# Attention core: one software pipeline per head pair in place of one per block of 256 queries

## The chip, the cores and the metric

The kernel runs as one program on all 8 cores of one Trainium2 chip. Each core works alone on two of the 16 sequences. The metric is the device time of the slowest core in microseconds, the median over several executions.

## What is computed

Three layers act on x, 16 sequences of 2048 x 1024, float32: `x + 0.5*ffn(layernorm(x))`, then `x + attn(layernorm(x))`, then `x + 0.5*ffn(layernorm(x))` with the same ffn weights. The ffn is itself an attention without a mask over 4 of 16 heads that a router picks. The change is in `attn`, differential attention with a causal mask:

```
q = rotary(rmsnorm(x @ Wq.T)); k = rotary(rmsnorm(x @ Wk.T))   # 16 heads of 64
v = x @ Wv.T                                                    # 8 heads of 128
attn = softmax(causal(q @ k.T / 8))                             # 2048 x 2048 for each of 16 heads
attn = attn[head 2h] - lam * attn[head 2h+1]                    # 8 pairs
out  = layernorm(attn @ v) * (1 - LAMBDA_INIT)
return out @ Wproj.T
```

## The kernel before

Five queues of instructions are written out in Python, one for each engine: `pe` (TensorE, the matmuls), `act` (ScalarE, the exponentials), `dve` (VectorE), `gps` (GpSimd) and `sp` (SyncE, which issues DMAs here). Each engine works through its own queue in order. What ties them together are counting semaphores: `P.wait("pe", self.ACT, n)` puts into TensorE's queue a wait until ScalarE has finished its n-th instruction, and everything behind that wait in TensorE's queue waits too.

For each of the two sequences a core runs the stages: load and layernorm, ffn, q/k/v projection, `emit_attn_core`, the output projection with the next layernorm, ffn again. `emit_attn_core` is the stage that the change touches.

It loops over the NH = 8 pairs p of heads. For each pair:

- SyncE loads the transposed q and k of the pair and its v strip, one pair ahead, into one of two halves (`issue_pair_loads`).
- The 2048 queries are cut into 8 blocks of 256, `qh` = 0 to 7. Because of the causal mask, block qh needs the keys of 2qh+2 tiles of 128, taken two tiles at a time: it has qh+1 groups g. So a pair has 1+2+...+8 = 36 groups, and the stage has 2 x 8 x 36 = 576 in all.
- One group is three steps. `emit_scores(g)`: TensorE writes the scores of 2 heads x 2 key tiles x 256 queries into one of two PSUM tiles, `pbig[g % 2]` (4 matmuls, and 4 short ones more that add the mask in the last, diagonal, group of a block). `emit_exp(g)`: one ACTIVATE on ScalarE turns these 1024 columns into probabilities in slot g % 4 of `big_b`. `emit_av(g)`: TensorE multiplies them with v (8 matmuls of 129 columns, 6 in the diagonal group) and accumulates in the banks `obs`, of which there are two sets that take turns from block to block.
- The order within a block is a pipeline two groups deep: scores 0, scores 1, exp 0, and then for each g: exp g+1, av g, scores g+2. Scores g+2 waits for exp g, which frees the PSUM tile. At the end of a block the pipeline runs empty: the next block's scores 0 stand in TensorE's queue behind av of the last group, and that waits for the last exp.
- After the block's last av, VectorE does the fixup (lines 1022 to 1038: two reciprocals, a scaling, and for each of two query tiles the difference of the two heads and its statistics). The av of the block after next waits for it (`fixup_ms`), since it writes the same banks. In every pair but the first, the first fixup also waits until the pair before has been stored (`store_ms`), since both use `zstrip`.
- At the end of a pair ScalarE computes 1/sqrt(var) (L1043, L1045), VectorE normalises 16 tiles (L1050), and SyncE stores them to `zhat_d`. ScalarE's first exp of the next pair stands behind L1045 in its queue.

In the profile's lines L954 is the score matmul, L963 the mask matmul, L974 the exp, L995 the av matmul.

Of the kernel before, what the change touches and what calls it, by code (L numbers as in the profile page):

```python
# [76 lines left out]
class MK:  # L77
# [823 lines left out]
    def emit_attn_core(self, b):  # L901
        P = self
# [15 lines left out]
        store_ms = None  # L918
        for p in range(NH):
# [9 lines left out]
            first_fix_of_pair = True  # L929
            for qh in range(8):  # L930
                o = qh % 2
                obs = (self.pb[2 * o], self.pb[2 * o + 1])
                oput = [0, 0]
                nkt = 2 * qh + 2
                ngroups = nkt // 2
                n_out = [0, 0]
                for kt in range(nkt):
                    for qi in range(2):
                        if 2 * qh + qi >= kt:
                            n_out[0] += 1  # L940
                            n_out[1] += 1

                def emit_scores(g):
                    kts = (2 * g, 2 * g + 1)
                    pw = self.pbig[g % 2]
                    P.wait("pe", self.ACT, exp_ms[g % 2])
                    diag = [(ki, qi) for ki, kt in enumerate(kts)
                            for qi in range(2) if 2 * qh + qi == kt]
                    for hi in range(2):
                        last_of_all = (hi == 1)  # L950
                        for ki, kt in enumerate(kts):
                            is_last = (not diag) and (ki == 1)
                            P.pe(lambda e, kt=kt, ki=ki, hi=hi, pw=pw, qh=qh,
                                 qT=qT, kT=kT, is_last=is_last: e.matmul(  # L954
                                pw[:, hi * 512 + ki * 256:hi * 512 + (ki + 1) * 256],
                                kT[hi * 64:(hi + 1) * 64, kt * 128:(kt + 1) * 128],
                                qT[hi * 64:(hi + 1) * 64, qh * 256:(qh + 1) * 256],
                                start=(ki == 0), stop=is_last,
                                tile_position=(hi * 64, 0)),
                                inc=(is_last and last_of_all))  # L960
                        for di, (ki, qi) in enumerate(diag):
                            is_last = (di == len(diag) - 1)
                            P.pe(lambda e, pw=pw, hi=hi, ki=ki, qi=qi, is_last=is_last: e.matmul(  # L963
                                pw[:, hi * 512 + ki * 256 + qi * 128:hi * 512 + ki * 256 + (qi + 1) * 128],
                                self.ident_bf, self.diag_bf,
                                start=False, stop=is_last),
                                inc=(is_last and last_of_all))
                    return self.PE.n

                def emit_exp(g, pe_ms):  # L970
                    pw = self.pbig[g % 2]
                    P.wait("act", self.PE, pe_ms)
                    P.wait("act", self.PE, av_ms.get(("pt", g % 4), 0))
                    P.act(lambda e, pw=pw, g=g: e.activation(  # L974
                        out=self.big_b[:, (g % 4) * 1024:(g % 4) * 1024 + 1024],
                        in_=pw[:, 0:1024], func=AF.Exp, scale=0.125, bias=self.neg8_col))
                    exp_ms[g % 2] = self.ACT.n
                    return self.ACT.n

                def emit_av(g, act_ms):  # L980
                    kts = (2 * g, 2 * g + 1)
                    P.wait("pe", self.ACT, act_ms)
                    if oput[0] == 0:
                        P.wait("pe", self.DVE, fixup_ms[o])
# [265 lines left out]
```

How the kernel before makes its waits and increments, by code:

```python
    def wait(self, eng, sem, val):  # L173
        if val > 0:
            self.q[eng].append(lambda e, s=sem, v=val: e.wait_ge(s.h, v))
# [15 lines left out]
    def dma(self, queue, out, in_, **kw):  # L191
        ch = self._chan(queue)
        v0 = ch.n
        self.on(queue, lambda e, o=out, i=in_, s=ch, w=v0, kw=kw: (
            e.wait_ge(s.h, w), e.dma_start(out=o, in_=i, **kw).then_inc(s.h, 16)))
        return ch, ch.inc(16)
# [1 line left out]
    def dmat(self, queue, out, in_):  # L198
        ch = self._chan(queue)
        v0 = ch.n
        self.on(queue, lambda e, o=out, i=in_, s=ch, w=v0: (
            e.wait_ge(s.h, w), e.dma_start_transpose(o, i).then_inc(s.h, 16)))
        return ch, ch.inc(16)
# [8 lines left out]
        def step(e, f=fn, s=sem, w=w):  # L212
            e.wait_ge(s.h, w)
            f(e).then_inc(s.h, 1)
# [12 lines left out]
    def pe(self, fn, inc=True):  # L227
        if inc:
            self.on("pe", lambda e, f=fn, s=self.PE: f(e).then_inc(s.h, 1))
            return self.PE.inc(1)
        self.on("pe", fn)
        return self.PE.n
```

## Time and profile before

| | |
|---|---|
| median of 3 runs | 4290.23 us (4281.84 to 4294.78) |
| the profiled execution | 4281.57 us |
| span of its slowest core, core 1 | 4280.0 us; all cores 4251.3 to 4280.0 us |
| busy on core 1: TensorE, ScalarE, VectorE | 2549.3 us (60%), 1468.1 us (34%), 1446.2 us (34%) |
| mean granted TensorE clock, core 1 | 0.684 of 2.4 GHz |
| attention core, first exp to end of last exp, core 1 | 967.8 to 1569.3 us and 3100.5 to 3688.8 us |
| exps in it (L974) | 576, 641.7 us busy, 673.6 us of idle time before them |

The profile is of the slowest core. A row of it gives an engine, a line, what the instruction writes and reads, how many there were, and the idle time of the engine just before them with what ended it. The granted clock is 1.00 or 0.50 (2.4 or 1.2 GHz) nearly everywhere; it is the share of TensorE's clock that the chip let through in that stretch.

### The profile page before, as it was taken

The page shows a single profiled execution, that of the slowest core. Times are in us where ns is not written, and L with a number is a line of the kernel's source. Part 1 is how long each engine was busy: PE and PEld are TensorE (multiplying, and loading weights), DVE is VectorE, ACT ScalarE, POOL GpSimd, SP SyncE. Part 2 cuts the span into 40 slices and gives each one's busy share as a digit, 9 for nine tenths or more (in the row PEclk, how much of TensorE's full clock was granted, in tenths as well). Part 3 has the DMA queues.
Part 4 walks back from the last instruction along what each step waited for, and adds up shares of the span by engine and source line. Part 5 has one row for each costly group of instructions (what it writes and reads, how often), then busy time and mean ns, then how long its engine had stood idle before and what let it go on. Part 6 is the DMA issues. An engine that isn't in the chain of part 4 may idle for free.

```text
span 4280.0 us, 55933 instructions; the slowest of 8 cores (4251.3 to 4280.0 us)
## 1 busy us (share of the span) xinstructions
PE 2549.3 (60%) x18326; PEld 1246.0 (29%) x18326; DVE 1446.2 (34%) x3373; ACT 1468.1 (34%) x1602; POOL 332.8 (8%) x258
## 2 busy tenths in 40 slices
PE   3277456456656647377732775564566565474876
PEld 0144212123333322144201442121233333222442
DVE  4121156623333335221241211566243433252212
ACT  1017323304555531017310173233055454310272
POOL 0000006610000000000000000066000000000000
PEclk8675558776777769675565855687777687786755
DMA  4500330042111130500235003300511211305003
GB/s 116 95 12 1 65 81 35 35 99 38 21 32 29 21 63 29 96 1 1 85 129 95 12 2 64 81 35 35 113 24 21 40 21 26 65 30 89 1 1 104
DMA packets 355659, 207.79 MB, mean 49 GB/s; under 512 B 292630, under 2 KB 301078, under 8 KB 355378
## 3 DMA queue, kind: packets, MB, share of 16 engines
q1 hardware_dynamic: 215570, 109.55, 9.9%
q0 software_dynamic: 26144, 44.31, 6.5%
q10 hardware_dynamic: 113664, 50.34, 5.1%
q8 instruction: 156, 2.56, 0.3%
q14 instruction: 125, 1.02, 0.1%
HBM read 114.20 MB, written 79.76 MB: 45 GB/s over the span
## 4 chain that ended last, share of the span: by engine, by line
PE 38%; DVE 19%; ACT 16%; DMA 10%; issue 9%; ACTq 4%; SPq 1%; DVEq 1%; POOL 0%; POOLq 0%
ACT big_b L974 7%; ACT big_b L608 7%; PE pw L995 6%; ACTq L202 4%; PE pw L954 4%; PE pw L628 4%; PE pw L690 3%; PE pw L539 3%; PE pw L1081 3%; PE pw L810 3%; PE pw L596 3%; PE pw L493 2%; DVE zstrip L1050 2%; PE pw L364 2%; PE pw L366 2%
## 5 line engine op out<-in xcount | busy, mean ns | idle before, releaser
L974 ACT ACTIVATE big_b<-pw,c 128x1024 bf16<-128x1024 f32 x576 | 641.7, 1114 | 673.6 <-PE pw L963 423.5
L608 ACT ACTIVATE big_b<-pw 128x1024 bf16<-128x1024 f32 x512 | 524.3, 1024 | 674.4 <-PE pw L596 649.6
L995 PE MATMUL pw<-vstrips,big_b 128*128 128x129 bf16 x4352 | 434.1, 256 | 434.8 <-ACT big_b L974 182.5
L995 PEld LDWEIGHTS pw<-vstrips,big_b 128*128 128x128 bf16 x4352 | 329.6, 114 | 567.9 <-issue 567.7
L787 PE MATMUL pw<-big_b,reg_a 128*128 128x512 bf16 x1024 | 281.4, 442 | 235.9 <-ACT scr L867 135.6
L628 PE MATMUL pw<-vstrips,big_b 128*128 128x65 bf16 x4096 | 306.2, 240 | 156.1 <-ACT big_b L608 100.5
L628 PEld LDWEIGHTS pw<-vstrips,big_b 128*128 128x128 bf16 x4096 | 236.0, 125 | 358.5 <-issue 358.5
L954 PE MATMUL pw<-qk_strm 64*128 64x256 bf16 x2304 | 320.5, 330 | 31.8 <-DMA vstrips<-vhat_d 31.8
L596 PE MATMUL pw<-qk_strm 64*128 64x256 bf16 x2048 | 296.2, 401 | 3.0 <-DVE vstrips L573 3.0
L329 ACT ACTIVATE scr<-x_res 128x1024 f32<-128x1024 f32 x96 | 101.4, 1057 | 406.6 <-DVE stats L327 327.2
L787 PEld LDWEIGHTS pw<-big_b,reg_a 128*128 128x128 bf16 x1024 | 110.1, 110 | 407.2 <-issue 327.1
L1022 DVE RECIPROCAL stats<-pw 128x2 f32<-128x2 f32 x128 | 21.8, 170 | 609.6 <-PE pw L995 540.0
L651 DVE RECIPROCAL stats<-pw 128x2 f32<-128x2 f32 x128 | 21.8, 170 | 608.5 <-PE pw L628 591.8
L364 PE MATMUL pw<-scr,c 128*1 128x512 f32 x128 | 84.7, 750 | 204.4 <-DVE qk_bf L362 108.7
L690 PE MATMUL pw<-qk_strm 128*128 128x512 bf16 x256 | 132.0, 620 | 124.6 <-issue 83.0
L810 PE MATMUL pw<-big_b,reg_a 128*128 128x512 bf16 x512 | 114.1, 386 | 123.4 <-DMA big_b<-attn_wvT 123.4
L1081 PE MATMUL pw<-wselg,big_b 128*128 128x512 bf16 x512 | 114.9, 388 | 80.9 <-DMA big_b<-zhat_d 41.1
L397 ACT COPY scr<-pw 1x512 f32<-1x512 f32 x4 | 2.3, 575 | 445.6 <-DMA reg_a<-lnx_d 445.6
L703 DVE SCALAR_TENSOR_TENSOR x_res<-pw,x_res 128x512 f32<-128x512 f32 x128 | 88.5, 691 | 186.5 <-PE pw L695 178.7
L954 PEld LDWEIGHTS pw<-qk_strm 64*128 64x128 bf16 x2304 | 101.3, 103 | 126.4 <-issue 80.1
L327 DVE TENSOR_REDUCE stats<-x_res 128x1 f32<-128x1024 f32 x96 | 117.1, 1219 | 22.8 <-DMA x_res<-x 13.8
L539 PE MATMUL pw<-reg_a,wselg 128*128 128x512 bf16 x512 | 120.3, 400 | 4.8 <-DVE rowbuf L525 4.8
(174 smaller groups left out, 2709.4 us busy)
## 6 DMA issues: line engine op xcount, KB each, us to landing
x_res<-x SPq DMA_DIRECT2D x32, 512.0 KB
y<-x_res SPq DMA_DIRECT2D x32, 512.0 KB
lnx_d<-pt ACTq DMA_DIRECT2D x48, 256.0 KB, 2.1
vstrips<-vhat_d SPq DMA_DIRECT2D x16, 516.0 KB
big_b<-ffn_wkT POOLq DMA_DIRECT2D x4, 2048.0 KB, 25.4
big_b<-ffn_wvT POOLq DMA_DIRECT2D x4, 2048.0 KB, 22.2
zhat_d<-zstrip SPq DMA_DIRECT2D x16, 512.0 KB
lnx_d<-qk_bf ACTq DMA_DIRECT2D x24, 256.0 KB, 2.1
```

The costliest lines, as they stand in the source:

```text
L202: e.wait_ge(s.h, w), e.dma_start_transpose(o, i).then_inc(s.h, 16)))
L539: P.pe(lambda e, h=h, qb=qb, fc=fc, bank=bank, base=base: e.matmul(bank[:, 0:512], self.wsel[:, base + fc * 256 + h * 128: base + fc * 256 ...
L596: P.pe(lambda e, hp=hp, qh=qh, kt=kt, ki=ki, hi=hi, pw=pw: e.matmul(pw[:, hi * 512 + ki * 256:hi * 512 + (ki + 1) * 256], self.ksel[hi * 6 ...
L608: P.act(lambda e, pw=pw, g=g: e.activation(out=self.big_b[:, (g % 4) * 1024:(g % 4) * 1024 + 1024], in_=pw[:, 0:1024], func=AF.Exp, scale= ...
L628: first=first, last=last: e.matmul(ob[:, qi * 65:(qi + 1) * 65], self.big_b[:, (g % 4) * 1024 + hi * 512 + ki * 256 + qi * 128: (g % 4) * ...
L690: P.pe(lambda e, tt=tt, half=half, c=c, bank=bank: e.matmul(bank[:, 0:512], zt[:, c * S + tt * 128:c * S + (tt + 1) * 128], wo[:, c * 1024 ...
L787: P.pe(lambda e, tt=tt, fc=fc, half=half, bank=bank, wb=wb: e.matmul(bank[:, 0:512], self.reg_a[:, fc * S + tt * 128:fc * S + (tt + 1) * 128],
L810: P.pe(lambda e, tt=tt, fc=fc, half=half, bank=bank, wb=wb: e.matmul(bank[:, 0:512], self.reg_a[:, fc * S + tt * 128:fc * S + (tt + 1) * 128],
L954: qT=qT, kT=kT, is_last=is_last: e.matmul(pw[:, hi * 512 + ki * 256:hi * 512 + (ki + 1) * 256], kT[hi * 64:(hi + 1) * 64, kt * 128:(kt + 1 ...
L974: P.act(lambda e, pw=pw, g=g: e.activation(out=self.big_b[:, (g % 4) * 1024:(g % 4) * 1024 + 1024], in_=pw[:, 0:1024], func=AF.Exp, scale= ...
L995: vst=vst, first=first, last=last: e.matmul(ob[:, qi * 129:(qi + 1) * 129], self.big_b[:, (g % 4) * 1024 + hi * 512 + ki * 256 + qi * 128: ...
L1081: P.pe(lambda e, tt=tt, fc=fc, half=half, bank=bank: e.matmul(bank[:, 0:512], self.big_b[:, fc * S + tt * 128:fc * S + (tt + 1) * 128], wp ...
```

## The change

The pipeline of groups no longer starts anew with each block. All 36 groups of a pair are put into one list `tasks` of (qh, g), and the steps run over its index i: exp i+1, av i, scores i+2. So while the last group of block qh is finished, the scores and the exp of the first groups of block qh+1 are already issued. What each block needs (its banks `obs`, the count of matmuls that have gone into them, `n_out`) moves into a dictionary `qst`. The choice of the PSUM tile and of the slot of `big_b` goes by a running number `gbase + i` in place of g. The fixup is unchanged and is issued after the av of a block's last group, which now means after the scores i+2 have been put into TensorE's queue. The number, shape and work of the instructions are the same; only the order in TensorE's and ScalarE's queues and the waits with them change. At the end of a pair the pipeline still runs empty.

The diff, cut to its core:

```diff
+        gbase = 0
         for p in range(NH):
...
+            tasks = [(qh, g) for qh in range(8) for g in range(qh + 1)]
+            qst = {}
             for qh in range(8):
                 o = qh % 2
-                obs = (self.pb[2 * o], self.pb[2 * o + 1])
-                oput = [0, 0]
...
+                qst[qh] = {"obs": (self.pb[2 * o], self.pb[2 * o + 1]),
+                           "oput": [0, 0], "n_out": n_out}
...
-                def emit_scores(g):
-                    kts = (2 * g, 2 * g + 1)
-                    pw = self.pbig[g % 2]
-                    P.wait("pe", self.ACT, exp_ms[g % 2])
+            def emit_scores(i):
+                qh, g = tasks[i]
+                gi = gbase + i
+                kts = (2 * g, 2 * g + 1)
+                pw = self.pbig[gi % 2]
+                P.wait("pe", self.ACT, exp_ms[gi % 2])
...
-                def emit_av(g, act_ms):
-                    kts = (2 * g, 2 * g + 1)
-                    P.wait("pe", self.ACT, act_ms)
-                    if oput[0] == 0:
-                        P.wait("pe", self.DVE, fixup_ms[o])
+            def emit_av(i, act_ms):
+                qh, g = tasks[i]
+                gi = gbase + i
+                sq = qst[qh]
+                obs, oput, n_out = sq["obs"], sq["oput"], sq["n_out"]
+                kts = (2 * g, 2 * g + 1)
+                P.wait("pe", self.ACT, act_ms)
+                if oput[0] == 0:
+                    P.wait("pe", self.DVE, fixup_ms[qh % 2])
...
-                G = ngroups
-                sc_ms = {0: emit_scores(0)}
-                if G > 1:
-                    sc_ms[1] = emit_scores(1)
-                e_ms = {0: emit_exp(0, sc_ms[0])}
-                pe_av = 0
-                for g in range(G):
-                    if g + 1 < G:
-                        e_ms[g + 1] = emit_exp(g + 1, sc_ms[g + 1])
-                    pe_av = emit_av(g, e_ms[g])
-                    if g + 2 < G:
-                        sc_ms[g + 2] = emit_scores(g + 2)
+            M = len(tasks)
+            sc_ms = {0: emit_scores(0)}
+            if M > 1:
+                sc_ms[1] = emit_scores(1)
+            e_ms = {0: emit_exp(0, sc_ms[0])}
+            for i in range(M):
+                if i + 1 < M:
+                    e_ms[i + 1] = emit_exp(i + 1, sc_ms[i + 1])
+                pe_av = emit_av(i, e_ms[i])
+                if i + 2 < M:
+                    sc_ms[i + 2] = emit_scores(i + 2)
+                qh, g = tasks[i]
+                if g != qh:
+                    continue
+                o = qh % 2
+                obs = qst[qh]["obs"]
                 P.wait("dve", self.PE, pe_av)
                 if first_fix_of_pair and store_ms is not None:
                     P.wait("dve", store_ms[0], store_ms[1])
...
+            gbase += M
```

## Rows read from the trace of the kernel before

**Rows 1.** The page's groups: busy, mean ns; idle before, by releaser.

```profile
L974 ACT ACTIVATE big_b<-pw,c 128x1024 bf16<-128x1024 f32 x576 | 641.7, 1114 | 673.6 <-PE pw L963 423.5
```

**Rows 2.** Windows from pair start to pair start: busy by engine, PEclk third from last.

```profile
967.80:1039.80 72.00, 51.65 (x448) 30.78 (x448) 23.39 (x88) 40.72 (x38) 0.00 (x0) 0.67 0.09 14
...
1195.40:1270.40 75.00, 46.14 (x448) 27.99 (x448) 28.41 (x104) 40.70 (x38) 0.00 (x0) 0.75 0.15 29
...
1421.70:1499.50 77.80, 50.45 (x448) 30.12 (x448) 28.42 (x104) 40.68 (x38) 0.00 (x0) 0.68 0.14 28
```

**Rows 3.** The same windows summed: 12 middle pairs; then first and last pairs.

```profile
sum 913.70, PE 570.03 PEld 343.81 DVE 341.03 ACT 488.63 POOL 0.00; mean PE 47.50 PEld 28.65 DVE 28.42 ACT 40.72 POOL 0.00
...
sum 276.10, PE 185.51 PEld 112.36 DVE 97.78 ACT 161.67 POOL 0.00; mean PE 46.38 PEld 28.09 DVE 24.44 ACT 40.42 POOL 0.00
```

**Rows 4.** Timeline, TensorE then ScalarE, end of block 4 at clock 0.50: start, duration.

```profile
1454.44 1.05 PE L995 MATMUL pw<-vstrips,big_b 128*128 128x129 bf16 x8
1455.42 0.61 PE L954 MATMUL pw<-qk_strm 64*128 64x256 bf16 x4
1455.98 1.03 PE L995 MATMUL pw<-vstrips,big_b 128*128 128x129 bf16 x8
...
1458.54 1.07 PE L995 MATMUL pw<-vstrips,big_b 128*128 128x129 bf16 x8
1460.22 0.81 PE L995 MATMUL pw<-vstrips,big_b 128*128 128x129 bf16 x6 [0.60 <-ACT big_b L974]
1460.96 1.04 PE L954 MATMUL pw<-qk_strm 64*128 64x256 bf16 x8
1463.15 1.02 PE L995 MATMUL pw<-vstrips,big_b 128*128 128x129 bf16 x8 [1.16 <-ACT big_b L974]
...
1458.96 1.11 ACT L974 ACTIVATE big_b<-pw,c 128x1024 bf16<-128x1024 f32 x1 [1.59 <-PE pw L963]
```

**Rows 5.** Timeline of ScalarE, then TensorE: block 7 at clock 1.00, next pair.

```profile
1101.67 2.32 ACT L974 ACTIVATE big_b<-pw,c 128x1024 bf16<-128x1024 f32 x2 [1.20 <-PE pw L954]
1104.20 5.96 ACT L974 ACTIVATE big_b<-pw,c 128x1024 bf16<-128x1024 f32 x5 [0.21 <-PE pw L954]
1111.00 1.11 ACT L974 ACTIVATE big_b<-pw,c 128x1024 bf16<-128x1024 f32 x1 [0.84 <-PE pw L963]
1117.85 1.11 ACT L974 ACTIVATE big_b<-pw,c 128x1024 bf16<-128x1024 f32 x1
...
1106.67 0.62 PE L995 MATMUL pw<-vstrips,big_b 128*128 128x129 bf16 x8 [0.26 <-ACT big_b L974]
1107.22 0.40 PE L954 MATMUL pw<-qk_strm 64*128 64x256 bf16 x4
```

**Rows 6.** Timeline, begin of pairs 1 and 3: store, fixup, first av of block 2.

```profile
1046.70 0.38 SPq L195 DMA_DIRECT2D zhat_d<-zstrip  x1
1052.98 0.17 DVE L1022 RECIPROCAL stats<-pw 128x2 f32<-128x2 f32 x1 [6.42 <-DMA zhat_d<-zstrip]
1056.76 0.18 DVE L1038 BATCH_NORM_AGGREGATE stats<-stats 128x2 f32<-128x6 f32 x1
...
1210.88 1.03 PE L995 MATMUL pw<-vstrips,big_b 128*128 128x129 bf16 x8 [7.92 <-DVE stats L1038]
```

**Rows 7.** Timeline of TensorE, pair 0 of the first sequence.

```profile
969.08 0.81 PE L995 MATMUL pw<-vstrips,big_b 128*128 128x129 bf16 x6 [1.41 <-ACT big_b L974]
...
976.40 1.02 PE L995 MATMUL pw<-vstrips,big_b 128*128 128x129 bf16 x8 [1.16 <-ACT big_b L974]
```

**Rows 8.** Windows at either clock, core 1: columns as in rows 2.

```profile
270.00:477.00 207.00, 163.07 (x1680) 92.27 (x1680) 32.63 (x112) 131.07 (x128) 0.97 (x2) 0.55 0.01 1
1230.30:1267.80 37.50, 24.48 (x293) 15.14 (x291) 10.43 (x40) 25.35 (x23) 0.00 (x0) 1.00 0.01 2
1431.00:1469.30 38.30, 26.93 (x197) 16.00 (x198) 14.62 (x55) 17.05 (x16) 0.00 (x0) 0.50 0.25 47
1609.80:1666.70 56.90, 56.85 (x256) 25.26 (x256) 38.90 (x45) 16.12 (x29) 0.00 (x0) 0.97 0.00 1
```

**Rows 9.** Windows of core 4, in the q/k projection.

```profile
628.50:668.00 39.50, 34.73 (x132) 13.86 (x129) 25.81 (x33) 14.13 (x23) 19.39 (x15) 0.81 0.09 34
```

More of the change, by code:

```diff
@@ new lines, in emit_scores @@
+            def emit_scores(i):
[4 more added lines that the diff above has]
+                P.wait("pe", self.ACT, exp_ms[gi % 2])
+                diag = [(ki, qi) for ki, kt in enumerate(kts)
+                        for qi in range(2) if 2 * qh + qi == kt]
+                for hi in range(2):
+                    last_of_all = (hi == 1)
+                    for ki, kt in enumerate(kts):
+                        is_last = (not diag) and (ki == 1)
+                        P.pe(lambda e, kt=kt, ki=ki, hi=hi, pw=pw, qh=qh,
+                             qT=qT, kT=kT, is_last=is_last: e.matmul(
+                            pw[:, hi * 512 + ki * 256:hi * 512 + (ki + 1) * 256],
+                            kT[hi * 64:(hi + 1) * 64, kt * 128:(kt + 1) * 128],
+                            qT[hi * 64:(hi + 1) * 64, qh * 256:(qh + 1) * 256],
+                            start=(ki == 0), stop=is_last,
+                            tile_position=(hi * 64, 0)),
+                            inc=(is_last and last_of_all))
+                    for di, (ki, qi) in enumerate(diag):
+                        is_last = (di == len(diag) - 1)
+                        P.pe(lambda e, pw=pw, hi=hi, ki=ki, qi=qi, is_last=is_last: e.matmul(
+                            pw[:, hi * 512 + ki * 256 + qi * 128:hi * 512 + ki * 256 + (qi + 1) * 128],
+                            self.ident_bf, self.diag_bf,
+                            start=False, stop=is_last),
+                            inc=(is_last and last_of_all))
+                return self.PE.n
@@ new lines, in emit_av @@
+            def emit_av(i, act_ms):
+                qh, g = tasks[i]
+                gi = gbase + i
+                sq = qst[qh]
[4 more added lines that the diff above has]
+                    P.wait("pe", self.DVE, fixup_ms[qh % 2])
+                for hi in range(2):
+                    ob = obs[hi]
+                    for ki, kt in enumerate(kts):
+                        for qi in range(2):
+                            if 2 * qh + qi < kt:
+                                continue
+                            first = (oput[hi] == 0)
+                            oput[hi] += 1
+                            last = (oput[hi] == n_out[hi])
+                            P.pe(lambda e, hi=hi, gi=gi, ki=ki, kt=kt, qi=qi, ob=ob,
+                                 vst=vst, first=first, last=last: e.matmul(
+                                ob[:, qi * 129:(qi + 1) * 129],
+                                self.big_b[:, (gi % 4) * 1024 + hi * 512 + ki * 256 + qi * 128:
+                                           (gi % 4) * 1024 + hi * 512 + ki * 256 + (qi + 1) * 128],
+                                vst[:, kt * 129:(kt + 1) * 129],
+                                start=first, stop=last), inc=last)
+                av_ms[("pt", gi % 4)] = self.PE.n
+                return self.PE.n
```

63 lines of the change are left out of this document (11 added, 52 removed).

## The prediction

> **What bounds the kernel now.** I read the page's costly groups first. The exp of the attention core stands on top: 576 instructions of 1114 ns, 641.7 us, with 673.6 us of idle time before them, ended by matmuls [rows 1]. So ScalarE has work for just over half of this stage, and what ends its waits is TensorE. Next the windows, cut at the first exp of each pair of heads: a pair takes around 75 us, ScalarE is busy for some 40.7 us of it and TensorE for 46 to 52 us [rows 2]. Neither engine is full: the stage is bound by a chain that hands work back and forth. The 12 middle pairs (pairs 1 to 6 of both sequences) add up to 913.7 us, the first and last pairs to 276.1 us, together 1189.8 us of the 4280 [rows 3].
>
> Then the timeline of single blocks, at both clocks.
>
> At clock 0.50, inside a block, TensorE goes from av to scores in 0.98 us and from scores to the next av in 0.56 us: 1.54 us a group with no wait between [rows 4]. TensorE is the bound there. At clock 1.00, five exps in a row take 5.96 us: 1.21 us from one to the next, of which 0.10 is the gap. TensorE goes from av to scores in 0.55 us, its four score matmuls end 0.40 us after that, and it waits 0.26 us for an exp before the av [rows 5]. ScalarE is the bound.
>
> At a block's end the pipeline runs empty, and this is what the reader is to see. At clock 0.50 TensorE waits 0.60 us for the last exp, and then 1.16 us for the first exp of the next block, whose scores were issued only behind the last av [rows 4]. At clock 1.00 ScalarE waits 1.20 us at the block's start and 0.21 us after two exps. Its 0.84 us ahead of the diagonal group is another thing: that group's scores have 4 matmuls more [rows 5].
>
> A pair's beginning has a wait of its own. The store of the pair before is issued at 1046.70, and the first fixup begins at 1052.98, when it has landed; it ends at 1056.94, and the first av of block 2 waits for it, because it writes the same banks. In pair 3, which starts at 1195.4, this av starts at 1210.88, 15.5 us into the pair, after 7.92 us of waiting [rows 2, 6].
>
> **The change part by part.** No instruction is added or removed. I sum what each boundary between blocks gives.
>
> (a) Boundary at clock 0.50. Before, from the av ahead of the last to the first av of the next block: 1458.54 to 1463.15, 4.61 us. In the new order TensorE has av (0.98), scores of the next block (0.56), the last av, scores again, av. The last exp ends at 1458.96 + 1.11 = 1460.07 and its av starts 0.15 later, at 1460.22 as before; it takes 0.74 (1460.22 to 1460.96), the scores 0.56, and the next av starts at 1461.52 with its exp long done, since that one needed only scores that ended near 1460.1. It gives 4.61 - 2.98 = 1.63 us.
>
> (b) Boundary at clock 1.00. The gaps of 1.20 and 0.21 become 0.10 each: 1.21 us. The diagonal gap of 0.84 stays, since scores i+2 still stand behind av i.
>
> (c) The boundaries ahead of block 2's first av, in 14 of 16 pairs: nothing. They are covered by the wait for the store [rows 6]. The store hangs on VectorE's L1050 of the pair before, which hangs on nothing that moves. TensorE still cannot pass this av, and the two exps that can run ahead are the same two. In the two first pairs there is no store to wait for. Before, the first av of block 2 is 976.40 - 969.08 = 7.32 us behind the first av [rows 7]. In the new order TensorE has av 0.75, diagonal scores 1.58 (0.56 and the 1.02 of four mask matmuls, as 1456.96 to 1458.54), av 0.98, scores 0.56, av 0.75, scores 0.56 between them: 5.2 us. It gives 2.1 us. If the store were not what holds them, the same 2.1 us would come in 14 more pairs.
>
> (d) What is late next. VectorE's fixup takes 3.96 us (1052.98 to 1056.94) [rows 6]; two in a row at a pair's start end about 4.1 us after block 2's first av, and block 3's first av, which needs the second, now comes 5.5 us after it (0.98 + 1.58 + 0.98 + 0.56 + 0.15 + 0.74 + 0.56). It is 1.4 us clear. From there a block lasts 6 us or more against 4 of fixup. If that cover were gone it would cost about 1 us a pair.
>
> (e) The pair's end: the last av, fixup, L1043, L1045, then the next pair's first exp: 1111.00 to 1117.85 [rows 5], the same.
>
> With five boundaries that count in each pair, two at 0.50 and three at 1.00: 2 x 1.63 + 3 x 1.21 = 6.9 us a pair, 16 pairs 110.4, and the first pairs' 2 x 2.1 on top: 114.6 us with the clock as it is.
>
> (f) The clock. In pair 3 it is 1.00 for the 37.5 us from 1230.3 to the end, and 0.50 for the other half (0.75 over the pair's 75.0 us) [rows 2, 8]. The rise comes 34.9 us into the pair, in block 4. In block 4 TensorE runs for 6.6 us without a wait, from the first av, one group ahead of 1454.44, to 1459.5 [rows 4]; in block 3, a group shorter, for 5.1, and in those before for less. In pair 6 the clock stayed at 0.50 through block 4 and rose only at 1469.3, 47.7 us in [rows 8]: this is why the middle pairs take 76.1 us on the average where pair 3 takes 75.0. With the new order TensorE has no wait over 0.2 us from the first av of block 2, 15.5 us into the pair. As bounds for the rise I take 5 us behind that av, a stretch like the one in which block 3 did not yet bring it, and 16.1 us, where block 4 has run as far as it had in pair 3 (19.4 less two boundaries). I take 10 us, near the middle. Over the 6.1 us between 10 and 16.1, a group costs 1.21 in place of 1.54: 6.1 x 0.33 / 1.54 = 1.3 us. And I take the late rises as gone, 76.1 - 75.0 = 1.1 us, as the long stretches are there in every pair now. A middle pair is then 75.0 - 6.9 - 1.3 = 66.8 us.
>
> The sum: 12 middle pairs 801.6 in place of 913.7, 112.1 us less. The two last pairs end with the last exp, 5.7 us short of a pair's length: 61.1 each. The two first pairs have block 2's first av at 6.5 in place of 15.5 us (969.08 - 967.80 + 5.2): 57.8 each. These four are 237.8 in place of 276.1, 38.3 less. Together 150.4 us. The profiled execution of 4281.6 us would be 4131.2. The median of the runs shown is 8.7 us above that execution; the same 150.4 off it gives 4139.8, and I say **4140 us**.
>
> **The rivals.**
>
> *The clock rises no earlier than now.* Only the boundaries give: 4290.2 - 114.6 = 4176. For it: in the ffn attention, where TensorE is busy for 163 of 207 us, the granted clock is 0.55 [rows 8], so being busy is not enough. Against it: its matmuls are of other shapes (65 columns a head), and here blocks 4 to 7 run at 1.00.
>
> *The wait for the store gives way too*, so that 2.1 us come in 14 more pairs: 4111. Only a store that lands earlier could do this, and nothing moves it.
>
> *A third clock.* In the q/k projection core 4 has 0.81 [rows 9], and core 1 never has it. If the denser stage brought 0.81 in place of 1.00, the way from one exp to the next but one (0.15 + 0.55 + 0.40 + 0.20 and an exp of 1.11, 2.41 us for two groups) would have 0.95 us of matmuls stretched to 1.17: 1.31 in place of 1.21 a group, 27 such groups in 16 pairs, 43 us: 4183. The Trainium skill (TensorE: Matmul & The Clock Gate, Part 1: The HAM clock gate) says that a peak-current limiter takes a whole die to 13/16 once three of its cores run dense matmuls; by that rule every core would have it here. The trace has this level in the projections alone, on one die, and not in this stage, where all cores have 1.00 at the same time.
>
> *The clock never leaves 0.50 in this stage.* The cost from block 2's first av: 32 groups of 1.54 and five diagonals of about 1 us, 54.3 us, and 6 for the end: 15.5 + 54.3 + 6 = 75.8, as now: 4290. For it: the ffn attention. It would need the whole stage to count as that one does.
>
> *The clock is lost for what follows too* (slower). The output projection has 256 matmuls in 56.9 us at 0.97 [rows 8]. If the gapless stage left TensorE at 0.50 up to its end, these would take twice as long: 2 x 57 = 114 us on top of a stage that gains nothing: 4404. It decides if the clock is at 0.50 from 1.6 ms to the layernorm. Nothing in the rows speaks for it but 0.55 in the ffn.
>
> **How the numbers follow.** The forecast has 0.74, the clock as now 0.12, the store 0.03, the third clock 0.04, no rise 0.05, the slower one 0.02. Around 4140: a rise at 5 us behind the av gives 1 us more a pair (4124), one at 16.1 takes 1.3 away (4161), and the runs shown lie 13 us apart. That makes 4112 to 4168 for the likeliest; up to 4180 it takes in the clock as now, and holds 0.8. About 0.3% is what a measurement of this kernel can tell from no change: faster 0.93, same 0.05, slower 0.02.
>
> **What the changed kernel's profile would show.** The idle time before the exps falls from 673.6 us to about 520 (with the 0.84 and the pair boundaries left). At a block's start the exps run on with gaps of 0.1 us; the 0.84 is there. Block 2's first av still comes 15 to 17 us into a pair, behind a fixup that a store released. Middle pairs take 66 to 68 us, and PEclk over a pair is above 0.75. I would be wrong if the clock stayed at 0.50 past block 4, if block 3's first av waited for VectorE, or if the windows fell by about 7 us a pair only.

## The result and the profile after

The changed kernel takes 4139.3 us (median of 8 runs, 4131.3 to 4148.0), the kernel before 4287.0 us (8 runs, 4274.7 to 4294.8). The ratio is 0.9658, with a 95% interval from 0.9642 to 0.9675: 147.7 us less by the medians. In some executions the cores of one die run longer at a lower granted clock; these (one each of `pool_norm` and `pool_norm_fill` below, and three of the kernel before beside them) are left out of all medians and ratios here.

The profiled execution took 4147.99 us; its slowest core is core 2, with a span of 4146.5 us. The profile's group of the exps, which answers to [rows 1]:

```profile
L978 ACT ACTIVATE big_b<-pw,c 128x1024 bf16<-128x1024 f32 x576 | 641.8, 1114 | 526.6 <-PE pw L966 453.8
```

The same work, 641.8 us, with 147.0 us less idle time before it. Now the windows of core 2 from pair start to pair start, as in [rows 2] and [rows 3]: a first pair, a middle one, the sum of the 12 middle pairs, and the sum of the four first and last ones.

```profile
966.00:1023.90 57.90, 42.71 (x452) 24.78 (x448) 23.40 (x88) 40.72 (x38) 0.00 (x0) 0.88 0.09 17
...
1156.30:1223.10 66.80, 43.23 (x448) 25.39 (x448) 28.41 (x104) 40.68 (x39) 0.00 (x0) 0.81 0.15 33
...
sum 803.80, PE 519.42 PEld 303.78 DVE 341.04 ACT 488.79 POOL 0.00; mean PE 43.28 PEld 25.32 DVE 28.42 ACT 40.73 POOL 0.00
...
sum 238.80, PE 171.35 PEld 100.22 DVE 97.79 ACT 161.59 POOL 0.00; mean PE 42.84 PEld 25.05 DVE 24.45 ACT 40.40 POOL 0.00
```

The attention core now takes 1042.6 us on this core in place of 1189.8 on core 1 [rows 3], and the rest of the kernel 3103.9 in place of 3090.2: the whole gain lies in the stage. By the medians over the eight cores of each execution the stage takes 1040.6 us in place of 1189.0. ScalarE is still idle for 26 of 67 us in a middle pair.

A boundary at clock 1.00, the timeline of ScalarE and then of TensorE around the end of block 3, beside [rows 5]:

```profile
1114.53 3.53 ACT L978 ACTIVATE big_b<-pw,c 128x1024 bf16<-128x1024 f32 x3 [0.84 <-PE pw L966]
1118.26 2.32 ACT L978 ACTIVATE big_b<-pw,c 128x1024 bf16<-128x1024 f32 x2 [0.21 <-PE pw L957]
1121.42 3.53 ACT L978 ACTIVATE big_b<-pw,c 128x1024 bf16<-128x1024 f32 x3 [0.84 <-PE pw L966]
...
1115.78 0.51 PE L1003 MATMUL pw<-vstrips,big_b 128*128 128x129 bf16 x6 [0.68 <-ACT big_b L978]
1116.22 0.40 PE L957 MATMUL pw<-qk_strm 64*128 64x256 bf16 x4
1117.10 0.62 PE L1003 MATMUL pw<-vstrips,big_b 128*128 128x129 bf16 x8 [0.48 <-DVE stats L1036]
1117.65 0.40 PE L957 MATMUL pw<-qk_strm 64*128 64x256 bf16 x4
```

The exp of block 3's diagonal group starts at 1114.53 and the two of block 4 follow it with gaps of 0.1 us: the 1.20 is gone. The gap of 0.21 is still there. The exp that it precedes needs the scores of 1117.65, and these stand behind the av of 1117.10, which waited for an exp. (The timeline puts this wait of 0.48 to VectorE; the exp ahead of it ended at 1116.85, 0.25 us before, and that is the usual distance between an exp and its av.)

A pair's beginning in the same pair at clock 0.50, TensorE and one exp, beside [rows 4] and [rows 6]:

```profile
1105.57 1.03 PE L1003 MATMUL pw<-vstrips,big_b 128*128 128x129 bf16 x8 [8.66 <-DVE stats L1050]
...
1108.12 1.07 PE L1003 MATMUL pw<-vstrips,big_b 128*128 128x129 bf16 x8
1109.12 0.61 PE L957 MATMUL pw<-qk_strm 64*128 64x256 bf16 x4
1109.79 0.81 PE L1003 MATMUL pw<-vstrips,big_b 128*128 128x129 bf16 x6
1110.53 0.61 PE L957 MATMUL pw<-qk_strm 64*128 64x256 bf16 x4
1111.32 0.62 PE L1003 MATMUL pw<-vstrips,big_b 128*128 128x129 bf16 x8 [0.18 <-DVE stats L1036]
...
1109.95 1.11 ACT L978 ACTIVATE big_b<-pw,c 128x1024 bf16<-128x1024 f32 x1 [0.31 <-PE pw L957]
```

Block 2's first av starts 15.4 us into the pair (1105.57 - 1090.18), after 8.66 us of waiting for a fixup: there the two joined boundaries gave nothing. (Over all cores this av stands at 15.6 us in the median of the 112 pairs with a store before them, and at 15.5 in the kernel before.) From it TensorE runs on into block 3. That pair's clock, by windows:

```profile
1090.20:1111.20 21.00, 10.82 (x74) 5.78 (x74) 11.21 (x40) 7.78 (x7) 0.00 (x0) 0.50 0.49 101
1111.20:1155.60 44.40, 31.55 (x374) 19.00 (x374) 17.22 (x65) 32.46 (x30) 0.00 (x0) 1.00 0.01 1
...
3426.30:3456.20 29.90, 19.21 (x136) 10.61 (x136) 15.17 (x55) 13.34 (x12) 0.00 (x0) 0.50 0.36 71
```

It rises 21 us into the pair, where pair 3 before had its rise at 34.9 [rows 8]. The last line is one of the late ones, 29.9 us. Over all 8 cores and their 112 pairs other than first ones, the clock's records have the rise at 35.2 us in the median before, with 23 pairs later than 40; now at 22.7 us, and none later than 34. As the rise I count the first one later than 10 us into a pair: in 21 of the 112 pairs now the clock also goes to 1.00 for 3.4 us before that.

### The profile page after: what moved, and what is told of

It is laid out like the page before. It is cut to its first block, busy times and chain, and to the rows that moved or that the text cites. A ratio compares the mean times of both kernels' runs of the same rounds, so it can differ in the third digit from the quotient of the medians.

```text
span 4146.5 us, 55933 instructions; the slowest of 8 cores (4094.4 to 4146.5 us)
## 1 busy us (share of the span) xinstructions
PE 2496.6 (60%) x18326; PEld 1197.6 (29%) x18326; DVE 1446.6 (35%) x3373; ACT 1468.1 (35%) x1602; POOL 333.1 (8%) x258
## 4 chain that ended last, share of the span: by engine, by line
PE 38%; DVE 19%; ACT 17%; DMA 9%; issue 9%; ACTq 5%; SPq 1%; DVEq 1%; POOL 0%; POOLq 0%
ACT big_b L608 7%; ACT big_b L978 7%; PE pw L1003 5%; ACTq L202 4%; PE pw L628 4%; PE pw L690 3%; PE pw L539 3%; PE pw L957 3%; PE pw L810 3%; PE pw L1094 3%; PE pw L596 3%; PE pw L493 3%; PE pw L366 2%; PE pw L364 2%; DVE zstrip L1063 2%
## 5 line engine op out<-in xcount | busy, mean ns | idle before, releaser
L978 ACT ACTIVATE big_b<-pw,c 128x1024 bf16<-128x1024 f32 x576 | 641.8, 1114 | 526.6 <-PE pw L966 453.8
L1003 PE MATMUL pw<-vstrips,big_b 128*128 128x129 bf16 x4352 | 389.1, 238 | 352.0 <-DVE stats L1050 123.4
L1003 PEld LDWEIGHTS pw<-vstrips,big_b 128*128 128x128 bf16 x4352 | 296.7, 106 | 482.7 <-issue 482.7
L628 PEld LDWEIGHTS pw<-vstrips,big_b 128*128 128x128 bf16 x4096 | 236.5, 125 | 357.9 <-issue 357.9
L957 PE MATMUL pw<-qk_strm 64*128 64x256 bf16 x2304 | 310.4, 301 | 31.1 <-DMA vstrips<-vhat_d 31.1
L596 PE MATMUL pw<-qk_strm 64*128 64x256 bf16 x2048 | 297.1, 402 | 3.0 <-DVE vstrips L573 3.0
L875 ACT ACTIVATE stats<-stats,c 128x16 f32<-128x16 f32 x64 | 19.7, 308 | 289.6 <-DVE stats L871 289.6
```

The costliest lines, as they stand in the source:

```text
L596: P.pe(lambda e, hp=hp, qh=qh, kt=kt, ki=ki, hi=hi, pw=pw: e.matmul(pw[:, hi * 512 + ki * 256:hi * 512 + (ki + 1) * 256], self.ksel[hi * 6 ...
L628: first=first, last=last: e.matmul(ob[:, qi * 65:(qi + 1) * 65], self.big_b[:, (g % 4) * 1024 + hi * 512 + ki * 256 + qi * 128: (g % 4) * ...
L957: qT=qT, kT=kT, is_last=is_last: e.matmul(pw[:, hi * 512 + ki * 256:hi * 512 + (ki + 1) * 256], kT[hi * 64:(hi + 1) * 64, kt * 128:(kt + 1 ...
L978: P.act(lambda e, pw=pw, gi=gi: e.activation(out=self.big_b[:, (gi % 4) * 1024:(gi % 4) * 1024 + 1024], in_=pw[:, 0:1024], func=AF.Exp, sc ...
L1003: vst=vst, first=first, last=last: e.matmul(ob[:, qi * 129:(qi + 1) * 129], self.big_b[:, (gi % 4) * 1024 + hi * 512 + ki * 256 + qi * 128 ...
```

## Experiments

Ten kernels, timed in four groups: the first four, then two, two and two. Each group ran on one chip, with runs of the kernel before beside it, and the ratios are against those. For the first four the stage itself is the sharper measure: the kernel before came out at 4302 us in that group (4281 to 4321), some 15 us above its median in the result, so their four ratios are probably a few tenths of a per cent too favourable. "The stage" is the attention core of both sequences on a run's slowest core, from the first exp to the end of the last, 1189.8 us before. It comes from one profiled execution of each kernel, and the eight cores of the kernel before lie between 1179 and 1197 us; so the difference of the medians over the eight cores is given beside it.

**Three parts of the change.** The changed kernel with only some boundaries joined. This is the edit; `JOINED` holds the blocks whose end is joined to the next block: (0, 1), (2, 3), or (4, 5, 6).

```diff
-            sc_ms = {0: emit_scores(0)}
-            if M > 1:
-                sc_ms[1] = emit_scores(1)
-            e_ms = {0: emit_exp(0, sc_ms[0])}
+            seg = [0]
+            for q in range(7):
+                seg.append(seg[-1] + (0 if q in JOINED else 1))
+            sg = [seg[qh] for qh, g in tasks] + [99, 99]
+            sc_ms, e_ms = {}, {}
             for i in range(M):
-                if i + 1 < M:
+                if i == 0 or sg[i] != sg[i - 1]:
+                    sc_ms[i] = emit_scores(i)
+                    if sg[i + 1] == sg[i]:
+                        sc_ms[i + 1] = emit_scores(i + 1)
+                    e_ms[i] = emit_exp(i, sc_ms[i])
+                if sg[i + 1] == sg[i]:
                     e_ms[i + 1] = emit_exp(i + 1, sc_ms[i + 1])
                 pe_av = emit_av(i, e_ms[i])
-                if i + 2 < M:
+                if sg[i + 2] == sg[i]:
                     sc_ms[i + 2] = emit_scores(i + 2)
```

`join_front`, expected:

> Only the boundaries between blocks 0, 1 and 2 are joined, the other five run empty as before. My theory: in 14 of 16 pairs the store wait covers them, so only the two first pairs get about 2 us shorter: 4 us in all, 0.999 of the time before, and the middle pairs stay at 76 us with block 2's first av 15 to 17 us in. Rival, the store does not hold them: about 2 us in every pair, 32 us, 0.993.

`join_mid`, expected:

> Only the boundaries 2 to 3 and 3 to 4 are joined. My theory: two boundaries of 1.4 us at clock 0.50 (45 us over 16 pairs), and the clock rises at 21 to 25 us of a pair instead of 35 or 48, which gives another 3 us a pair: together about 93 us, 0.978. Rival, the clock rises early only if the whole pair is one pipeline: 45 us, 0.990, and the rise stays at 35 us or later.

`join_back`, expected:

> Only the boundaries 4 to 5, 5 to 6 and 6 to 7 are joined. My theory: three boundaries of 1.10 us at clock 1.00 (53 us over 16 pairs) and a few us for the falls of the clock in block 6 that vanish, about 57 us, 0.987; the clock still rises at 35 or 48 us. With the other two runs the savings should add up to the whole change's 148 us. Rival, the clock carries the gain and boundaries at full clock give little: under 20 us, 0.996.

Measured: 0.9959 (0.9937 to 0.9981), 0.9791 (0.9753 to 0.9830) and 0.9829 (0.9792 to 0.9866); medians 4284.9, 4211.6 and 4228.4 us. The sums of the stage's two windows, in this order:

```profile
sum 1185.60, PE 756.89 PEld 452.66 DVE 439.22 ACT 650.24 POOL 0.00; mean PE 378.45 PEld 226.33 DVE 219.61 ACT 325.12 POOL 0.00
```

```profile
sum 1123.00, PE 721.47 PEld 432.34 DVE 438.79 ACT 650.43 POOL 0.00; mean PE 360.74 PEld 216.17 DVE 219.40 ACT 325.21 POOL 0.00
```

```profile
sum 1126.80, PE 748.26 PEld 445.61 DVE 439.18 ACT 649.88 POOL 0.00; mean PE 374.13 PEld 222.81 DVE 219.59 ACT 324.94 POOL 0.00
```

The stage is 4.2, 66.8 and 63.0 us shorter, 134 us together against 147 for all boundaries at once (by the medians over the cores 4.7, 71.3 and 64.0, 140 together against 148). The front boundaries give the 4 us expected and not 32. The ratio of that run lies between the two expectations and can't tell them apart, and 4 us are less than the cores differ by, but the pairs can: over all cores the first pairs take 66.7 us in place of 68.8, with block 2's first av 6.7 us into them in place of 8.6, while the middle pairs take 76.0 us both times and have that av at 15.5. The back boundaries give a little more than their 53 to 57 us. The middle ones give less than 93. Here the clock rises early but does not stay, as one pair of that run shows:

```profile
1181.30:1202.70 21.40, 11.46 (x81) 6.41 (x82) 11.40 (x41) 7.96 (x8) 0.00 (x0) 0.50 0.47 99
1202.70:1216.30 13.60, 9.28 (x113) 5.70 (x112) 6.59 (x25) 10.05 (x10) 0.00 (x0) 1.00 0.01 3
1216.30:1219.80 3.50, 3.50 (x30) 2.28 (x31) 1.65 (x6) 2.32 (x3) 0.00 (x0) 0.51 0.00 0
1219.80:1226.60 6.80, 4.08 (x51) 2.57 (x50) 1.44 (x6) 4.58 (x5) 0.00 (x0) 1.00 0.00 0
```

21.4 us into the pair it goes to 1.00, and in the blocks behind, whose boundaries still run empty, it falls back. In all 112 pairs of that run it rises (21.6 us in the median) and it falls back to 0.50 more than twice a pair on the average, where the changed kernel has about one fall. So the parts depend on each other: the early rise pays in full only if the boundaries after it are joined too. The rise itself does not need the whole pair in one pipeline; that rival is out.

**The clock without the new order.** To see whether idle time alone holds the clock down, `fill` leaves the order of the kernel before and adds matmuls that compute nothing in TensorE's wait ahead of each block's first av.

```diff
                     kts = (2 * g, 2 * g + 1)
-                    P.wait("pe", self.ACT, act_ms)
                     if oput[0] == 0:
                         P.wait("pe", self.DVE, fixup_ms[o])
+                        for _ in range(8):
+                            P.pe(lambda e, vst=vst, ob=obs[0]: e.matmul(
+                                ob[:, 0:129], self.ident_bf, vst[:, 0:129],
+                                start=True, stop=True), inc=False)
+                    P.wait("pe", self.ACT, act_ms)
```

> The kernel before, all boundaries left running empty, with 8 additional matmuls (identity times a v tile, into a bank that the block's first av overwrites) ahead of each block's first av, in the 1.16 us in which TensorE waits for the first exp. They compute nothing. My theory: TensorE's idle gaps keep the clock down, so with the gap filled the clock rises at 21 to 28 us of a pair though each boundary still costs what it did: about 3.5 us a pair, 55 us, 0.987. Rival, the clock follows the order of the real work, or the 0.60 us gap is enough to hold it down: no change, 1.000. Second rival, the added matmuls delay the av: slower by 128 x 0.1 us or more, 1.003.

Measured: 0.9873 (0.9837 to 0.9908), 4248.6 us. The clock in one pair (it starts at 1103.5), and the sum of the stage, by windows:

```profile
1113.70:1130.60 16.90, 9.44 (x73) 6.43 (x74) 8.77 (x33) 3.74 (x4) 0.00 (x0) 0.50 0.52 97
1130.60:1175.10 44.50, 32.20 (x394) 20.51 (x391) 13.26 (x50) 30.77 (x28) 0.00 (x0) 1.00 0.01 2
...
sum 1154.10, PE 776.97 PEld 503.81 DVE 438.57 ACT 649.93 POOL 0.00; mean PE 388.49 PEld 251.90 DVE 219.28 ACT 324.97 POOL 0.00
```

The rise is 27 us into this pair, 25 in the median (and in 102 of the 112 pairs the clock is at 1.00 for 3.4 us before that, at 6 to 8 us). More matmuls, and the stage is 35.7 us shorter. The boundary is still there. The timeline at one, at clock 1.00, TensorE with the additional matmuls of L985, and the exp; then TensorE at block 2's first av, L999, at clock 0.50:

```profile
1151.43 0.63 PE L985 MATMUL pw<-vstrips,cbf 128*128 128x129 bf16 x8
1151.50 4.74 ACT L974 ACTIVATE big_b<-pw,c 128x1024 bf16<-128x1024 f32 x4 [1.19 <-PE pw L954]
...
1120.49 1.03 PE L985 MATMUL pw<-vstrips,cbf 128*128 128x129 bf16 x8 [9.75 <-DVE stats L1042]
1121.31 1.07 PE L999 MATMUL pw<-vstrips,big_b 128*128 128x129 bf16 x8
```

So here idle time of TensorE keeps the clock down, and not the order of the real work. It gave less than the 55 us expected: block 2's first av stands behind its 8 additional matmuls too, 0.8 us at clock 0.50 and after the store's wait, where nothing hides them. That is the second rival, in this one place: an estimate of about 11 us, from 14 pairs x 0.8. By the medians over the cores the stage is 43.5 us shorter (1145.5 against 1189.0), and the 11 are what is missing there; the slowest core, with 35.7, has 8 us more that no run explains.

**The store wait.** The first fixup waits for the store of `zstrip`'s first half, but writes the second half. The wait is needed only ahead of the normalisation. In `before_mv` and `after_mv` it stands there.

```diff
-                if first_fix_of_pair and store_ms is not None:
-                    P.wait("dve", store_ms[0], store_ms[1])
-                    first_fix_of_pair = False
...
             P.wait("dve", self.ACT, av2)
+            if store_ms is not None:
+                P.wait("dve", store_ms[0], store_ms[1])
             for qt in range(NT):
```

> The kernel before with VectorE's wait for the previous pair's store moved from the pair's first fixup to the normalisation at the pair's end (L1050), the first instruction that writes the half of zstrip which the store reads. Boundaries run empty. My theory of what covers the first boundaries: the store's landing. Without it the first fixup starts when L1050 of the pair before ends, 6.8 us into the pair, and block 2's first av comes at about 10.8 us instead of 15.5: 4.7 us in 14 pairs, 66 us, 0.985. Rival, something else holds block 2 (the next pair's loads, TensorE): no change, 1.000.

> The changed kernel with the same move of the store wait. My theory: block 2's first av is then bound by VectorE (16 normalisations and a fixup, 10.8 us) and still not by the first two boundaries, so the same 4.7 us in 14 pairs, 66 us less than the changed kernel: 4073 us, 0.950 of the time before. Rival, the joined pipeline is freed further and the first boundaries now count too: 2 us a pair more, 0.943. Second rival, TensorE's shorter rest changes the clock: the pair's rise comes 4.7 us earlier with it in my theory; a clock that stays up over the pair's start would give 3 us a pair more.

Measured: 0.9849 (0.9806 to 0.9892), 4227.6 us, and 0.9502 (0.9458 to 0.9545), 4077.0 us. TensorE's timeline at block 2's first av, first in `before_mv`, in a pair that starts at 1035.64, then in `after_mv`, in a pair that starts at 1029.96:

```profile
1046.60 1.02 PE L995 MATMUL pw<-vstrips,big_b 128*128 128x129 bf16 x8 [3.38 <-DVE stats L1035]
...
1040.92 1.02 PE L1003 MATMUL pw<-vstrips,big_b 128*128 128x129 bf16 x8 [4.23 <-DVE stats L1047]
```

And the sum of the stage:

```profile
sum 983.30, PE 695.96 PEld 406.34 DVE 439.23 ACT 650.30 POOL 0.00; mean PE 347.98 PEld 203.17 DVE 219.61 ACT 325.15 POOL 0.00
```

The av comes at 10.96 us in both, as expected for VectorE's 16 normalisations and one fixup, and still waits for VectorE. The stage of `after_mv` is 59 us shorter than the changed kernel's 1042.5. The gain is nearly the same in either order of the pipeline (59.4 and 62.3 us by the medians, both a little under the 66 expected), so it doesn't hang on the change. The rival of `before_mv`, no change, is out, and so is the first of `after_mv`: its 0.943 lies outside the interval, and the front boundaries are covered still, now by VectorE. As for the second, the clock is at 0.50 at the start of every pair but the first ones, and its rise moved from 22.7 to 18.7 us, by about what the av moved.

**VectorE's normalisations on GpSimd.** To uncover the front boundaries, `pool_norm` gives the 16 normalisations to GpSimd.

```diff
+                P.wait("dve", self.GPS, norm_ms.get(2 * qh + 1, 0))
                 for qi in range(2):
                     qt = 2 * qh + qi
...
+            P.wait("gps", self.ACT, av2)
             if store_ms is not None:
-                P.wait("dve", store_ms[0], store_ms[1])
+                P.wait("gps", store_ms[0], store_ms[1])
             for qt in range(NT):
-                P.dve(lambda e, qt=qt: e.tensor_scalar(
+                norm_ms[qt] = P.gps(lambda e, qt=qt: e.tensor_scalar(
...
-            P.wait("sp", self.DVE, self.DVE.n)
+            P.wait("sp", self.GPS, self.GPS.n)
```

`pool_norm_fill` has in addition 16 matmuls of 512 columns ahead of each pair's first av:

```diff
+            P.wait("pe", self.DVE, fixup_ms[0])
+            for _ in range(16):
+                P.pe(lambda e, vst=vst, ob=self.pb[0]: e.matmul(
+                    ob[:, 0:512], self.ident_bf, vst[:, 0:512],
+                    start=True, stop=True), inc=False)
             e_ms = {0: emit_exp(0, sc_ms[0])}
```

> The changed kernel with the store wait moved, and the 16 normalisations at a pair's end (L1050 of the kernel before) given to GpSimd, which is idle in this stage; each fixup waits only for the two tiles that it overwrites. The work is the same. My theory: after the store, VectorE's 6.6 us of normalisations are what makes block 2's first av late (10.8 us into a pair). Without them it comes at about 6.5 us, as in a first pair: 4.3 us in 14 pairs, 60 us less than after_mv: about 4017 us, 0.936 of the time before. Rival, GpSimd takes so much longer for a tile, or slows VectorE so much, that the fixups wait for it: no gain over after_mv (0.950) or worse.

> The same, and 16 additional matmuls of 512 columns ahead of each pair's first av, where TensorE otherwise waits some 5 us for the fixup of the pair before; they compute nothing and are overwritten. My theory: this idle time is what brings the clock to 0.50 at each pair's start, so with it filled the clock stays at 1.00 in most pairs, and the groups up to the former rise (about 9 of them) take 1.21 instead of 1.5 us: 2 to 3 us a pair, 30 to 50 us, about 3975 us, 0.927 of the time before. Rival, the clock falls all the same, and at 0.50 the added matmuls last 6.8 us and delay the first av by 1 to 2 us: slower than pool_norm by 20 us.

Measured: 0.9486 (0.9459 to 0.9513), 4062.4 us, and 0.9468 (0.9427 to 0.9509), 4059.0 us. Both missed their expectations of 0.936 and 0.927, and are hardly better than `after_mv`. The stage of `pool_norm`, by windows on its slowest core, core 2:

```profile
sum 909.20, PE 668.79 PEld 392.90 DVE 369.45 ACT 649.98 POOL 177.64; mean PE 334.40 PEld 196.45 DVE 184.73 ACT 324.99 POOL 88.82
```

What GpSimd did there, by groups of instructions:

```profile
L1066 POOL TENSOR_SCALAR zstrip<-zstrip,stats 128x128 bf16<-128x128 bf16 x256 | 203.0, 793 | 929.0 <-ACT stats L1058 887.3 <-POOL zstrip L1066 41.7
```

The stage shrank by 74.1 us against `after_mv`, more than the 60 expected: block 2's first av stands at 6.9 us in place of 11.0, and the clock rises at 12.6 in place of 18.7. A tile takes 0.79 us on GpSimd. The fixups don't wait for it. What changes is the end of the stage: the load of the output projection's weights stands in GpSimd's queue behind all normalisations. GpSimd's timeline in `pool_norm` and in `after_mv`, on core 1 of each:

```profile
1440.16 0.95 POOL L195 DMA_DIRECT2D wselg<-attn_wpT  x1
```

```profile
877.77 0.89 POOL L195 DMA_DIRECT2D wselg<-attn_wpT  x1
```

The load is issued 562 us later. The rest of the kernel grew by most of what the stage gave: from 3092.7 us on the slowest core (4076.0 - 983.3) to 3155.8 (4065.0 - 909.2).

Where this time goes can be read behind the last exp. On core 1 the output projection's first matmul starts 71.2 us after that exp's end in `pool_norm` and 41.5 in `after_mv`, and the second sequence has 66.9 and 37.0. The pieces of the chain that ends in this matmul, the landing of the last store and the start of the matmul, in `pool_norm` and in `after_mv`:

```profile
1440.35 13.05 DMA zhat_d<-zstrip
...
1489.88 2.29 PE pw L1099 x5
```

```profile
1475.40 4.97 DMA zhat_d<-zstrip
...
1504.17 1.86 PE pw L1093 x4
```

The last pair's 16 tiles take longer on GpSimd, so that store is issued 21.7 us behind the last exp in place of 12.7: 9 us. The other 21 lie between the store and the matmul (49.5 us in place of 28.8). The load had landed at 1459.2, long before the matmul. But it was issued beside the store, at 1440.16, and so was the ffn's weight load, at 1441.11, which stands behind it in the queue; in `after_mv` that one went out at 1463.94, 11.5 us ahead of the store. With both next to it the store took 13.05 us to land in place of 4.97, and SyncE spent 16.6 us on one of the reads of `zhat_d` behind it, in place of at most 3.5. That the loads and the store got in each other's way is the likely reason, but is not shown; no run separates the two loads, or the loads from the late tiles.

`pool_norm_fill` did to the clock half of what was expected. It is at 1.00 for 90% of the stage in place of 78, and in 49 of the 112 pairs throughout. But it was worth 0.8 us in a middle pair (56.7 in place of 57.5), not 2 to 3, and the first pairs, which have no wait to fill, grew from 57.4 to 61.6 us. By the medians over the cores the stage is 2.5 us shorter than in `pool_norm`, and the time can't be told from it.

**That load first.** `pool_wfirst` puts the load at the start of the stage and, in the same edit, leaves the last pair's normalisations, which nothing hides, on VectorE. `pool_wfirst_fill` adds the 16 matmuls again, in all pairs but the first.

```diff
     def emit_attn_core(self, b):
         P = self
+        P.dma("gps", self.wselg[:, 0:8192].rearrange("p (c f) -> p c f", f=D), self.w["attn_wpT"].rearrange("(c p) f -> p c f", p=128))
...
+            ne, nop = ("dve", P.dve) if p == NH - 1 else ("gps", P.gps)
```

> pool_norm with the load of the output projection's weights put ahead of the normalisations in GpSimd's queue (in pool_norm it stood behind them all and was issued at 1440 instead of 878 us), and the last pair's normalisations left on VectorE. My theory: pool_norm's stage is 74 us shorter than after_mv's (907 against 981 us) and the rest 54 us longer, all of it the late load and the last pair's 16 tiles at 0.96 us on GpSimd. With both mended the rest is back at 3073 us: about 3985 us, 0.929 of the time before. Rival, GpSimd's work in the stage slows something else: the rest stays above 3100 us, 0.94 or more.

> The same, with the 16 additional matmuls ahead of the first av of every pair but the first (they compute nothing). In pool_norm_fill the middle pairs took 56.7 in place of 57.4 us, but the first pairs 62 in place of 57. My theory: 0.8 us in 12 middle and 1.5 in 2 last pairs, 12 us less than pool_wfirst, 0.926; no more, because the clock had already risen 6 to 13 us into the pair. Rival: no difference that can be measured, or slower.

Measured: 0.9341 (0.9277 to 0.9405), 4018.7 us, and 0.9299 (0.9246 to 0.9352), 4000.1 us. The rest of the kernel, on the slowest core, is back at 3102.6 us (4014.2 - 911.6), 10 us above `after_mv`'s 3092.7. On core 1 the output projection's first matmul comes 43.9 us after the last exp, and the store lands in 6.1 us. The 3985 us expected were too few mainly because the 3073 in them was a median over the cores, and the time is that of the slowest. The rival had the rest above 3100 us, 0.94 or more. The interval holds 0.94, and the rest is at its edge. Ten microseconds lie within what the rest differs by with nothing changed in it (3090.2 before, 3103.9 after), so whether GpSimd costs something more stays open. The sum of the stage without and with the additional matmuls, and one pair with them:

```profile
sum 911.60, PE 671.39 PEld 395.11 DVE 368.86 ACT 650.32 POOL 178.38; mean PE 335.69 PEld 197.55 DVE 184.43 ACT 325.16 POOL 89.19
```

```profile
sum 896.10, PE 688.30 PEld 399.60 DVE 370.28 ACT 650.31 POOL 177.48; mean PE 344.15 PEld 199.80 DVE 185.14 ACT 325.16 POOL 88.74
...
1150.30:1205.80 55.50, 41.61 (x464) 24.30 (x464) 23.50 (x88) 40.70 (x38) 12.67 (x16) 1.00 0.21 39
```

In this pair the clock is at 1.00 throughout. It is so in about half of the pairs, and the additional matmuls give 15.5 us in the stage (13.8 by the medians over the cores), near the 12 expected. The two intervals overlap, but both are against the same runs of the kernel before; the four runs with the matmuls (3994 to 4006 us) all lie below the four without (4011 to 4022).

## Why the prediction was right

The forecast was 4140 us, the median is 4139.3. That is closer than its terms were, and the closeness is luck, so here they are one by one.

**The boundaries (steps a, b).** The mechanism is shown by the timelines, and by `join_back` and `join_mid`; both sizes were somewhat too high. (b) At 1.00 I had 1.21 us: the 1.20 fell to 0.10, but the 0.21 stayed, so it is 1.10. Step (b) took the second gap for a consequence of the first; it comes from the scores standing behind an av that waits for its exp, and that order is the same inside the joined pipeline. (a) At 0.50 I had 1.63 us, with "the next av starts at 1461.52 with its exp long done". It is not: block 3's first exp starts at 1109.95, behind the scores of 1109.12, and ends at 1111.06, and its av starts 0.26 us later, 1.53 us after the diagonal av; step (a) had 1.30 there (0.74 + 0.56). That is 0.23 us less a boundary, 1.40. So the boundaries are worth 2 x 1.40 + 3 x 1.10 = 6.1 us a pair where I had 6.9.

**What covers the first ones (step c).** Right, and shown twice: block 2's first av still came 15.4 us in, and `join_front` shortened the first pairs alone, by the 2.1 us each that step (c) has. In the changed kernel that av stands at 6.7 us in them, where the sum had 6.5. `before_mv` shows that it is the wait for the store: without it the av moves from 15.5 to 11.0 us, where VectorE's normalisations hold it.

**What is late next (step d).** Right: VectorE's timeline in the pair shown has the last operation of its first and of its second fixup:

```profile
1105.24 0.18 DVE L1050 BATCH_NORM_AGGREGATE stats<-stats 128x2 f32<-128x6 f32 x1
...
1109.31 0.18 DVE L1050 BATCH_NORM_AGGREGATE stats<-stats 128x2 f32<-128x6 f32 x1
```

The second ends at 1109.49, and block 3's first av came at 1111.32, with 1.8 us to spare.

**The clock (step f).** The direction was right and is shown by `fill`: with the boundaries as before, filling the wait alone brings the rise from 35 to 25 us. The size was somewhat too small. I took the rise 10 us behind block 2's first av; it came 7 behind it (22.7 us into a pair in the median, the av at 15.4). With 3 us more at 1.21 in place of 1.54 that is an estimate of 0.6 us a pair, and in some pairs the boundary 3 to 4 has moved to clock 1.00. No run tells this term from the boundaries' by itself. That the late rises would be gone (1.1 us a pair) holds: none is later than 34 us.

**The sum.** 12 middle pairs: 803.8 us, forecast 801.6. First and last pairs: 238.8, forecast 237.8. The boundaries gave 0.8 us a pair less and, by what is left of the measured pair, the clock about as much more; that the two misses cancel is luck. The median of before turned out 3 us lower than the one that I started from, and the saving 147.7 where I had 150.4.

**The rivals.** The clock as now (4176) is out: the rise moved by 12.5 us in the median, and no pair is later than 34 us where before all but one were later than 30. The store giving way (4111) is out by block 2's av; it needed an edit of its own. The third clock did not come: no core has 0.81 in this stage, or anywhere in this execution, though each of the eight is at 1.00 for about 64% of the stage. By the limiter of the Trainium skill (TensorE: Matmul & The Clock Gate, Part 1: The HAM clock gate) a die goes to 13/16 once three of its cores run dense matmuls; the trace does not show it here. It doesn't refute it either: each core's times count from its own first instruction, so the rows can't show that the cores are in the stage at the same time, as the prediction had it. And the level does come to this stage in other executions. `join_front` has it on cores 2 to 5 and `pool_wfirst_fill` on cores 6 and 7. A stretch of core 5 in `join_front`, and ScalarE in it:

```profile
1078.80:1104.20 25.40, 18.60 (x200) 11.22 (x199) 5.85 (x22) 17.84 (x17) 0.00 (x0) 0.81 0.01 2
...
1096.29 2.32 ACT L979 ACTIVATE big_b<-pw,c 128x1024 bf16<-128x1024 f32 x2 [0.32 <-PE pw L958]
1098.83 2.33 ACT L979 ACTIVATE big_b<-pw,c 128x1024 bf16<-128x1024 f32 x2 [0.22 <-PE pw L958]
```

Two exps take 2.54 us from start to start (1098.83 - 1096.29), 1.27 a group; the rival had 1.31. So the level can come in this stage, and no run shows what decides it. No rise is out by PEclk, 0.76 to 0.88 in the pairs of the stage, and a clock lost for what follows by the output projection, whose first 256 matmuls ran at 0.98:

```profile
1525.00:1585.00 60.00, 56.69 (x256) 25.25 (x256) 41.51 (x48) 17.43 (x31) 0.00 (x0) 0.98 0.00 1
```

## What to carry to other kernels

A pipeline that runs empty at the end of each inner block costs the whole way through it each time; read it from the idle time ahead of a block's first instruction, and don't count the blocks that another wait covers. Where TensorE's gaps are what holds its clock at 0.50, closing them pays twice, but the later gaps must be closed too. And before work is given to an idle engine, look at what else stands in its queue, and at what its last piece holds up: of 74 us won in the stage 63 were lost behind it, where the last tiles came late and two weight loads were issued beside the store that everything waited for.

## What the runs showed that I had not expected

A wait can guard more than it needs to. The first fixup waited for a store that reads the half of `zstrip` which no fixup writes; moving that one wait to the normalisation, with no other change, gave 62 us on top of the change (4139.3 to 4077.0). Matmuls that compute nothing made the kernel before faster by 1.3%, because the granted clock of the useful ones rose 10 us earlier in a pair. The best version tried, `pool_wfirst_fill`, takes 4000.1 us, 0.9299 of the kernel before; without the matmuls that compute nothing it is 4018.7 us.
